# Both score bursts of the next chunk ahead of the first own terms, and four key units between the two own terms, in chunks 1 and 2 of a TTT recurrence

## The reference

```python
def step(S, inp):                      # one chunk of 16 tokens, all batches and heads
    qi, ki, vi, ei = inp
    kh = jnp.einsum('bchd,bhde->bche', ki, S)            # state product
    target = vi - ki
    mu = jnp.mean(kh, -1, keepdims=True)
    rstd = jax.lax.rsqrt(jnp.var(kh, -1, keepdims=True) + EPS)
    kh_hat = (kh - mu) * rstd
    g = w * kh_hat + b - target
    gw = g * w
    v_new = (gw - mean(gw) - kh_hat * mean(gw * kh_hat)) * rstd
    A = jnp.einsum('bchd,bshd->bhcs', qi, ki)            # scores
    A = jnp.where(tri, A, 0.0) * eta
    qh = jnp.einsum('bchd,bhde->bche', qi, S) - jnp.einsum('bhcs,bshe->bche', A, v_new)
    o = qi + _ln(qh, w, b)
    S = S - jnp.einsum('bchd,bche->bhde', ki * ei[..., None], v_new)
    return (S, o)
# cross attention
k = rmsnorm((encoder_hidden_states @ Wk).reshape(B, Skv, H, D), gk)
```

## Time and profile before

| | |
|---|---|
| median of 3 runs | 380.12 us (378.19 to 382.46) |
| profiled execution | 379.22 us |
| its span in the trace | 377.5 us |
| granted clock of PE, mean | 0.983 of full speed |
| PE busy | 337.9 us, 89% |
| DVE busy | 264.6 us, 70% |
| ACT busy | 202.0 us, 53% |
| instructions | 11630 |

### The profile page before, as it was taken

How to read it: one execution, slowest core, us unless ns; L and a number is a source line. 1 busy time by engine, 2 the same in 40 slices (tenths; PEclk the granted TensorE clock), 3 DMA queues, 4 the chain that set the end, 5 groups by cost and what they waited for, 6 DMA issues and landing times.

```text
span 377.5 us, 11630 instructions
## 1 busy us (share of the span) xinstructions
PE 337.9 (89%) x5083; PEld 240.2 (64%) x5083; DVE 264.6 (70%) x537; ACT 202.0 (53%) x372; POOL 75.7 (20%) x91
## 2 busy tenths in 40 slices
PE   1999997996978785998999999999999999999974
PEld 1544585564534422687697796887977969866732
DVE  0499988897799899647263764855857739567795
ACT  1245974864545474346426555555565566576351
POOL 3009300000000000000062441522714405300100
PEclk9999999999999899799999999999999999999998
DMA  8997000000501203270040200200202000000000
GB/s 199 278 285 255 4 4 3 3 5 3 170 3 39 92 2 114 49 128 3 0 108 10 55 2 16 58 0 16 57 4 66 3 15 2 2 16 1 16 1 28
DMA packets 17987, 19.97 MB, mean 53 GB/s; under 512 B 3712, under 2 KB 15376, under 8 KB 17680
## 3 DMA queue, kind: packets, MB, share of 16 engines
q1 hardware_dynamic: 17328, 18.69, 18.3%
q10 hardware_dynamic: 608, 0.54, 0.7%
HBM read 18.04 MB, written 1.18 MB: 51 GB/s over the span
## 4 chain that ended last, share of the span: by engine, by line
PE 75%; DVE 13%; ACT 5%; issue 4%; DMA 1%; SPq 0%; POOLq 0%; POOL 0%; DVEq 0%; ACTq 0%
PE ps L795 14%; PE ps L729 14%; PE ps L550 6%; PE ps L772 5%; PE ps L787 5%; PE ps L665 4%; PE ps L503 3%; PE ps L814 3%; PE ps L841 2%; PE ps L745 2%; PE ps L531 2%; PE ps L521 2%; PE ps L620 2%; PE ps L763 2%; PE ps L655 2%
## 5 line engine op out<-in xcount | busy, mean ns | idle before, releaser
L729 PEld LDWEIGHTS ps<-x1t,xwq 128*128 128x128 f32 x512 | 59.2, 192 | 6.0 <-issue 4.2
L729 PE MATMUL ps<-x1t,xwq 128*128 128x128 f32 x512 | 62.1, 278 | 0.5 <-ACT x1t L1196 0.5
L795 PE MATMUL ps<-mvo,cxp 128*128 128x256 f32 x224 | 51.8, 383 | 0.5 <-ACT cxp L1207 0.5
L1909 POOL TENSOR_SCALAR rstd<-mv 128x1 f32<-128x1 f32 x20 | 4.4, 220 | 209.8 <-DVE mv L1650 209.8
L795 PEld LDWEIGHTS ps<-mvo,cxp 128*128 128x128 f32 x224 | 41.3, 190 | 6.6 <-ACT cxp L1207 0.8
L665 PE MATMUL ps<-ctxt,xwk 128*128 128x512 f32 x64 | 35.0, 656 | 3.9 <-ACT kt L1079 2.7
L1159 ACT ACTIVATE qt<-ps 128x512 f32<-128x512 f32 x32 | 19.1, 597 | 32.3 <-PE ps L729 32.3
L1077 ACT ACTIVATE ksq<-ps 128x512 f32<-128x512 f32 x32 | 19.0, 592 | 20.2 <-PE ps L665 13.3
L1079 ACT ACTIVATE kt<-ps,gks 128x512 f32<-128x512 f32 x32 | 21.9, 686 | 0.0
L1166 ACT ACTIVATE qsq<-ps 128x512 f32<-128x512 f32 x32 | 19.0, 593 | 4.7 <-PE ps L745 4.6
L772 PEld LDWEIGHTS ps<-kt,qt 128*64 128x64 f32 x512 | 16.2, 138 | 6.8 <-ACT qt L1159 3.8
(11 more groups left out here) (238 smaller groups left out, 681.3 us busy)
## 6 DMA issues: line engine op xcount, KB each, us to landing
rkb<-kscale SPq DMA_DIRECT2D x16, 256.0 KB, 4.1
ctx<-in_ctx_dram SPq DMA_DIRECT2D x4, 512.0 KB, 7.5
xwo<-in_L_xattn_Wo_dram SPq DMA_DIRECT2D x1, 2048.0 KB, 14.2
xwq<-in_L_xattn_Wq_dram SPq DMA_DIRECT2D x4, 512.0 KB, 4.4
w1n<-in_L_ffn_w_gate_up_dram SPq DMA_DIRECT2D x1, 1408.0 KB, 9.7
xwv<-in_L_xattn_Wv_dram SPq DMA_DIRECT2D x1, 1024.0 KB, 11.3
xwk<-in_L_xattn_Wk_dram SPq DMA_DIRECT2D x1, 1024.0 KB, 16.4
xn<-in_x_dram SPq DMA_DIRECT2D x2, 512.0 KB, 6.0
```

What stands on the lines that cost most here:

```text
L729: last = mm(bank(n % 2, P, t * P), xwq[qn][:, k * BANK + t * P:k * BANK + (t + 1) * P], x1t[:, (i % 2) * D + k * P:(i % 2) * D + (k + 1) * ...
L795: last = mm(bank(turn_banks[turn_of[("y", i, 0)]], D), context_of(i)[:, h * P:(h + 1) * P], mvo[:, h * D:(h + 1) * D], start=h == 0, stop= ...
```

## The change

In chunks 1 and 2 PE now runs, behind the state products: scores (c+1,0), one key unit, scores (c+1,1), own terms (c,0), four key units, own terms (c,1). Before, it ran scores (c+1,0), one key unit, own terms (c,0), one key unit, scores (c+1,1), two key units, own terms (c,1), one key unit. Each chunk keeps its nine key units. On ACT the roots of a chunk's second half now stand behind five key units of the chunk instead of four, and the square of the gated output behind all nine instead of eight. Chunk 3 keeps its order; only the table's form differs.

```diff
-KEY_PLACES = [(1, 2), (2, 2, 1, 1, 2, 1), (2, 2, 1, 1, 2, 1), (2, 3, 3, 3)]
+KEY_PLACES = [(1, 2), (2, 2, 1, 4), (2, 2, 1, 4), (2, 2, 1, 3, 3)]
...
                 if c < NCH - 1:
                     scores_ttt(c + 1, 0)
-                    keys(next(places))
+                keys(next(places))
+                if c < NCH - 1:
+                    scores_ttt(c + 1, 1)
                 own_terms(c, 0)
-                if c < NCH - 1:
-                    keys(next(places))
-                    scores_ttt(c + 1, 1)
                 keys(next(places))
                 own_terms(c, 1)
                 for n in places:
...
-                keys(places[1])
+                keys(places[1] + places[2])
                 output_root(2 * c - 1)
                 state_root(c, 1)
-                for n in places[2:-2]:
-                    keys(n)
-                keys(places[-2])
+                keys(places[3])
                 gated_square(c - 1)
-                if c < NCH - 1:
-                    keys(places[-1])
```

## The result

The changed kernel takes 386.43 us (median of 4 runs, 385.17 to 390.28) against 379.76 us for the kernel before on the same chips. The ratio is 1.024, 95% interval 1.019 to 1.029: slower by 7 to 11 us. The medians, 6.7 us apart, are over all runs, while the ratio is over the fast ones alone, so the two differ by some 2 us. The forecast was 384.5 us in a range of 381.2 to 389.0. The profiled execution took 387.55 us, its span 385.8.

A forecast was written before the change was run, and what follows sets the result against it. PE was taken to be bound by instruction fetch, at least 3.7 us per 256 instructions, with DVE the other limit. The 4.4 us delay at state products (3,0) made 379.22 into 383.6, plus 0.9 for the median: 384.5, range 381.2 to 389.0.

The forecast's parts named there:

- The bound: PE in the recurrence, 59 to 146 us: starved by instruction fetch, one block per 256 instructions; DVE the other limit.
- The floor of 3.7 us: PE's instruction fetch: a block of 256 takes at least 3.7 us however fast its instructions are.
- Own terms (1,0) late and hidden: Chunk 1: PE stalls 2.5 us, own terms end at 87.4, nearly 4 us later, hidden under DVE's read at 89.16.
- Four key units before own terms (1,1), request held: Chunk 1: third unit waits for ACT until 92.7; own terms end at 95.3, or 96.6 if that holds the request.
- State products (2,0): Directly behind own terms (1,1): end at 99.3 or 100.4 instead of 98.11; delay 1.2 to 2.3 us, 2.3 taken.
- Chunk 2: Boundaries at 109.1, 112.8, 116.5; own terms (2,1) end at 124.5, state products (3,0) at 128.3, DVE's read 4.4 us later.
- rival 1: Chunk 2: packet asked for at 123.9 caught in the xwq load until its end, 3.3 us more; about 388, chance 0.25.
- The sum: Whole kernel: 4.4 us later at DVE's read of state products (3,0), carried to the end; 384.5 us.
- The signs: New profile: listed stall at own terms (1,0), boundary times, DVE's waits, and its read of state products (3,0) at 127 to 130.
- the two signs of being wrong: PE in the new profile: own terms (1,1) end before 94.1, or stalls leave the multiples of 256 instructions.
- No change: PE's fetch is not per-block latency but a pace set by something else; 380 us, chance 0.16.
- faster: Four key units cover the fetch, own terms (1,1) start at 90, DVE's waits go; 3.6 us gained, 376.5, chance 0.07.

The follow-up runs named there:

- the doubled scores: Kernel before the change with scores (2,1) issued twice in a row to the same place, 256 more instructions; 385.28 us, ratio 1.012 (1.006 to 1.018).

## Why the prediction was right, and where its sizes were off

- *The bound.* Right. Blocks of 256 instructions, one fetch each: the doubled scores show it by themselves. The floor of 3.7 us was a little high. The doubled scores have 3.45, and the trace of the kernel before has 3.46 itself (112.53 to 115.99).
- *Own terms (1,0) late and hidden.* Right: the stall in front of them is 1.91 us (2.5 forecast), and DVE reads them at 90.22, without waiting for PE.
- *Four key units before own terms (1,1), request held.* Right, and better supported than it was. Two values were given for the end of these terms, 95.3 and 96.6. They ended near 96.3, just before DVE's read at 96.44. The forecast had one unit waiting for ACT, until 92.7; two waited, until 92.40.
- *State products (2,0).* 2.3 us later forecast, 2.0 measured in the profile.
- *Chunk 2.* The boundaries forecast at 109.1 and 116.5 came at 109.42 and 116.54, so the interval of 5.92 us was indeed given back. Then two terms were too small. The four key units were taken at 4.9 us and took 6.17. Most of this goes with the half clock: ACT began to square the first unit 2.1 us after its start, where a unit runs 1.1 us at full clock, and ACT's pace sets the rest. Own terms (2,1) were due at 124.5 and read at 126.38, 1.9 us later; besides the 1.3 us of the units, the own terms ahead of them ran at half clock too (1.11 us for 42 records, 0.67 in rows 6). And the block for state products (3,0), due at 127.6, came at 131.47. Of those 3.9 us, 1.6 are the later boundary (125.5 for 123.9) and 2.9 the load, by the run without it; 0.6 is given back, since the fetch without the load takes 3.1 us from there and not 3.7.
- *The load.* This was rival 1, at 388 with a chance of 0.25. Its mechanism is what happened. Its time lies as near as the forecast's: the median of 386.43 is 1.9 above 384.5 and 1.4 below 387.8. The step that failed is the choice between the two. The forecast had the packet start at 125, half a microsecond into the load, and get through. The load began at 125.1 (124.5 forecast), but the boundary came only near 125.5, 1.6 us late, so that the request fell into the load.
- *The sum.* 4.4 us forecast; 6.7 between the medians, 8.3 between the spans, 9.0 (7.1 to 11.0) by the ratio. The time lies inside the range because the range was wide: the size of the loss was forecast at about half. By terms, at DVE's read of state products (3,0), 8.6 us later: 4.4 forecast, 1.9 for the later end of own terms (2,1), and 2.3 for the load, less what the quicker fetch gave back.
- *The signs.* Four were missed. DVE waited 3.72 us for own terms (1,1), not over 4. The stall at own terms (1,0) was 1.91 us, not 2.5, and ended at 84.98, not 85.9. The third boundary came 6.9 us after the second, not 5.6 to 6.8. DVE read state products (3,0) at 132.58, not between 127 and 130, and this is the one that matters. Neither of the two signs of being wrong came.
- *No change, and faster.* Both out: the stalls stayed 256 instructions apart, and own terms (1,1) began at 93.51, not at 90.

What stays open: how much the half clock costs by itself was not tried. And why a wait in the first part of a block holds the packet is not known. The traces show only that a packet starts about 1 to 2 us behind a boundary when nothing waits and no load runs, and 1.1 to 1.2 us after the wait has ended when something does; that 41 records in a wait still held it and 46 records in it did not rests on one place each.

## What to carry to other kernels

Where small matmuls come in bursts, count instructions, not busy time: here each 256 cost about 3.5 us or more, and long instructions were what hid a fetch. Put them where the engine downstream waits, but keep a semaphore wait out of the first part of a block (here the first 41 records), and look at which work the next boundary falls into. Look also at what a large load meets: here it cost nothing where DVE had time in hand, and about 3 us where DVE waited for the next block.

## What the runs showed that I had not expected

How much the load would cost: about 3 us of DVE's time in the changed kernel, from a load whose first use is at 165.7 us. PE also came back at half clock from some stalls: four key units took 6.17 us where the forecast had 4.9. And the score burst, which looks like the heart of the change, costs nothing that can be measured in its new place once two of the four key units stand behind the second own terms.
